# Gated delta attention and soft mixture on one core: biases forward, dispatch ahead, combination weights turned by DMA and in half precision

## The chip, the core and the metric

The kernel runs on one core of one Trainium2 chip. TensorE multiplies and transposes, VectorE, ScalarE and GpSimd work elementwise, SyncE issues DMAs. The metric is the device time of one execution in microseconds (us), here the median of three executions. Sources and views of the profile shorten the engines to PE, DVE, ACT, POOL and SP.

## The reference, cut to what matters

The input x is 4 x 2048 x 256. Two layers follow one another, each with a residual.

```python
# 1: gated delta attention on layernorm(x); per token, state S is 128 x 128
q, k, v = xn @ Wq + bq, normed(xn @ Wk + bk), xn @ Wv + bv
a, b, g = sigmoid(xn @ Wa + ba), sigmoid(xn @ Wb + bb), sigmoid(xn @ Wg + bg)
S = S @ (a * (I - b * k k^T)) + b * v k^T ;  o = (q S) * g ;  x1 = x + o @ Wo + bo
# 2: soft mixture on layernorm(x1), rms-normed: xn (2048 x 256), slots se (1024 x 256)
logits   = xn @ se.T                         # per batch 2048 x 1024
dispatch = softmax(logits, over tokens) ;    slots = dispatch.T @ xn
P        = gelu(slots @ w1) @ w2             # 1024 x 256
combine  = softmax(logits, over slots) ;     out = x1 + combine @ P
```

## The kernel before, in words

Everything is float32 in meaning. Wide products are made of half-precision pairs: each operand is split in a high and a low half-precision part, and three products (high x high, high x low, low x high) are summed in PSUM.

**Attention.** Tokens are taken in 16 chunks of 128, all four batches together. A step of the software pipeline (`step(i, q)`, run for i from -4) does the last work on chunk i and earlier work on chunks i+1 to i+4. A 16 x 16 diagonal part of each chunk's system is solved on VectorE by 15 pairs of small instructions (`product` L569, `column` L580), on data that go out to DRAM and come back (`M_dram`, `Mrep`, on SyncE's queue). Between the pairs, `biases` (L532) move the projections of chunk i+3 from PSUM into SBUF; TensorE's `queries` (L1060) and ScalarE's key norms wait for all four of them. At pair 10 `weights` (L614) makes PT, which TensorE's `heads` (L1176, L1177) wait for; ScalarE's `keys` (L879) wait for `heads`, and from them come the system matrix and the next DMA.

**Mixture.** Four batches run one after the other. Per batch TensorE does, in this order: logits of the first 512 slots (16 tiles of 128 tokens, `first_half`), logits of the second 512; `dispatch` of the first and of the second 512 slots (16 tiles each, 12 matmuls of 257 columns a tile, L1811); the two-layer expert (`hidden` L1837, `processed` L1851) for slot halves 0 and 1; then the combination: per tile of 128 tokens 8 transposes (`turn`, L1862) and 24 matmuls (`combine`, L1873). ScalarE copies each logits tile to L (L1620); VectorE updates the column maxima (L1457) and makes the row maxima (L1459). For dispatch, a tile passes VectorE (`shifted` L1481: L minus the column maxima, into Dm), ScalarE (`exps` L1640), ScalarE (`high_exps` L1647) and VectorE (`low` L1489). `turn_maxima`/`column_maxima`/`spread_maxima` reduce the column maxima and spread them over partitions, through TensorE, VectorE and TensorE again.

For the combination, ScalarE takes the exponential of a float32 row tile of L (`weights` L1680, into Ec), TensorE turns it in float32 into two PSUM banks, ScalarE copies the high half-precision part out (`high` L1686, Th), and VectorE subtracts for the low part (`low_weights` L1579, Tl). VectorE's `finish` (L1585, L1589) divides by the sum and adds x1. The x1 tiles and the results travel on SyncE's queue (`results`, L1402 to L1412), behind the reload of the dispatch operand X for the next batch (`load_X`, 32 DMAs).

The order of the work on each engine is written out by hand; there is no scheduler.

## Time and profile before

| | us |
|---|---|
| three executions | 1281.29, 1282.22 (median), 1282.69 |
| profiled execution | 1286.53 |
| its span, first to last instruction | 1284.7 |
| mean granted clock of TensorE | 0.977 of full speed |
| TensorE matmul busy | 1175.3 (91%) |
| VectorE busy / ScalarE busy / GpSimd busy | 906.5 / 727.6 / 240.9 |

Attention takes the first 509 us or so, and from one step to the next 27.5 us pass; the four batches of the mixture take 193.4, 193.2, 193.6 and 195.5 us. GpSimd is at work in the attention alone. Busy shares overlap, and an engine's mean is an average over stages with different limits, so the stage has to be read.

### The profile page before, as it was taken

To read this page: it belongs to the slowest core of one execution; us is meant where nothing else is said; L and a number is where in the kernel's file an instruction comes from. 1 tells how busy PE (TensorE), PEld (TensorE's weight loads), DVE (VectorE), ACT (ScalarE), POOL (GpSimd) and SP (SyncE) were. 2 spreads that over 40 slices of the span, in tenths; PEclk is the share of its full clock that TensorE was granted. 3 is DMA by queue.
4 is the path that set the end of the run, shared out by engine and by line. 5 is a ranking of instruction groups with operands and counts; after the bars stand their busy time and mean duration, and the time that the engine had idled before them with its cause. 6 is when DMAs were issued, how large, how long until landed. Compare 5 with 4: busy or idle time off the path is not lost.

```text
span 1284.7 us, 26863 instructions
## 1 busy us (share of the span) xinstructions
PE 1175.3 (91%) x8600; PEld 894.9 (70%) x8600; DVE 906.5 (71%) x2131; ACT 727.6 (57%) x1369; POOL 240.9 (19%) x275
## 2 busy tenths in 40 slices
PE   3599889989999978999999999999999999999999
PEld 2377767777777766467788467788467788466788
DVE  4568778888878874998445998445998445997444
ACT  3445555655555623578654478654478654477654
POOL 3445544556544540000000000000000000000000
PEclk9789999999999987999999999999999999999999
DMA  5113332232332124330212030212030212000012
GB/s 176 35 35 79 88 84 66 66 75 75 91 91 66 51 69 96 94 73 17 59 54 70 1 66 15 60 54 70 1 66 13 62 50 74 8 2 1 1 50 73
DMA packets 122044, 73.09 MB, mean 57 GB/s; under 512 B 50048, under 2 KB 119680, under 8 KB 121984
## 3 DMA queue, kind: packets, MB, share of 16 engines
q1 hardware_dynamic: 120656, 71.74, 20.7%
q8 instruction: 41, 0.67, 0.2%
q10 hardware_dynamic: 1264, 0.53, 0.2%
q14 instruction: 19, 0.16, 0.0%
q0 software_dynamic: 64, 0.00, 0.0%
HBM read 38.16 MB, written 25.69 MB: 50 GB/s over the span
## 4 chain that ended last, share of the span: by engine, by line
PE 47%; DVE 17%; issue 12%; DMA 8%; ACT 5%; SPq 4%; DVEq 1%; POOL 1%; ACTq 0%; POOLq 0%
PE m_wide L1873 13%; DMA Mrep<-M_dram 7%; PE m_wide L1851 7%; PE m_wide L1837 6%; SPq L285 4%; PE m_wide L1862 4%; PE m_wide L1758 4%; DVE m_Dm L1481 4%; DVE rmax L1459 2%; DVE cmax L1457 2%; ACT m_Eh L1647 2%; PE m_wide L1811 2%; DVE Zc L580 2%; DVE m_El L1489 2%; PE a_bank L1060 2%
## 5 line engine op out<-in xcount | busy, mean ns | idle before, releaser
L1811 PE MATMUL m_wide<-m_X,m_Eh 128*128 (+1 forms) x1024 | 172.5, 273 | 16.5 <-DVE m_El L1489 16.4
L1758 PE MATMUL m_wide<-seT,XT 128*128 128x512 f16 x672 | 147.3, 379 | 0.8 <-issue 0.8
L1873 PE MATMUL m_wide<-m_Ph,m_Th 128*128 128x257 f16 x512 | 140.4, 274 | 1.7 <-DVE m_Pl L1520 1.7
L1811 PE MATMUL m_wide<-m_X,m_El 128*128 128x257 f16 (+1 forms) x512 | 139.7, 273 | 0.0
L1873 PE MATMUL m_wide<-m_Ph,m_Tl 128*128 128x257 f16 x512 | 139.4, 272 | 0.0
L1873 PE MATMUL m_wide<-m_Pl,m_Th 128*128 128x257 f16 x512 | 139.1, 272 | 0.0
L1579 DVE TENSOR_TENSOR m_Tl<-m_wide,m_Th 128x1024 f16<-128x1024 f32 x64 | 78.4, 1224 | 71.4 <-ACT m_Th L1686 70.9
L1811 PEld LDWEIGHTS m_wide<-m_X,m_Eh 128*128 128x128 f16 x1024 | 97.7, 98 | 40.0 <-DVE m_El L1489 19.7
L1758 PEld LDWEIGHTS m_wide<-seT,XT 128*128 (+1 forms) x672 | 65.6, 98 | 78.1 <-issue 1.1
L1686 ACT CAST m_Th<-m_wide 128x1024 f16<-128x1024 f32 x64 | 64.7, 1011 | 86.1 <-PE m_wide L1862 86.1
L1620 ACT COPY L<-m_wide 128x512 f32 (+1 forms) x112 | 65.4, 587 | 84.3 <-PE m_wide L1758 84.0
L1640 ACT ACTIVATE m_E<-m_Dm,m_eshift 128x512 f32<-128x512 f32 x128 | 92.0, 722 | 31.8 <-DVE m_Dm L1481 30.6
L1489 DVE TENSOR_TENSOR m_El<-m_E,m_Eh 128x512 f16<-128x512 f32 x128 | 87.6, 687 | 9.5 <-ACT m_Eh L1647 5.9
L1481 DVE TENSOR_TENSOR m_Dm<-L,m_Mb 128x512 f32<-128x512 f32 x128 | 86.8, 684 | 1.4 <-ACT m_E L1640 1.4
L1851 PE MATMUL m_wide<-w2s,m_hh 128*128 128x256 f16 x512 | 84.3, 273 | 0.0
L1457 DVE TENSOR_TENSOR cmax<-cmax,L 128x512 f32<-128x512 f32 x112 | 77.0, 688 | 6.3 <-ACT L L1620 5.3
L1837 PE MATMUL m_wide<-m_sTh,w1s 128*128 128x512 f16 x256 | 77.6, 379 | 0.8 <-ACT m_E L1657 0.8
L1514 DVE TENSOR_TENSOR m_hl<-m_E,m_hh 128x512 f16<-128x512 f32 x64 | 43.6, 691 | 48.2 <-ACT m_hh L1668 48.2
L1647 ACT CAST m_Eh<-m_E 128x512 f16<-128x512 f32 x128 | 76.5, 604 | 0.0
L1459 DVE TENSOR_REDUCE rmax<-L (+1 forms) x112 | 75.9, 678 | 0.0
L1680 ACT ACTIVATE m_Ec<-L,m_nrm 128x1024 f32 (+1 forms) x64 | 73.6, 1150 | 0.3
L1851 PE MATMUL m_wide<-w2s,m_hl 128*128 128x256 f16 x256 | 69.8, 273 | 0.0
(187 smaller groups left out, 2628.5 us busy)
## 6 DMA issues: line engine op xcount, KB each, us to landing
L<-in_L_attn_x_dram SPq DMA_DIRECT2D x16, 512.0 KB, 7.4
Mrep<-M_dram SPq DMA_DIRECT2D x16, 512.0 KB
x_dram<-x SPq DMA_DIRECT2D x16, 512.0 KB, 7.4
m_X<-X_dram SPq DMA_DIRECT2D x128, 64.0 KB, 1.8
m_x1t<-x_dram SPq DMA_DIRECT2D x64, 128.0 KB, 2.1
out_dram<-m_o SPq DMA_DIRECT2D x64, 128.0 KB, 1.7
X_dram<-Xh SPq DMA_DIRECT2D x16, 256.0 KB, 2.3
X_dram<-Xl SPq DMA_DIRECT2D x16, 256.0 KB, 2.3
```

The lines of the kernel that those rows point to most:

```text
L1457: dve.tensor_tensor(cmax[:, half_at], cmax[:, half_at], L[:, z, bass.ds(tile, 1), :] .rearrange("q a n -> q (a n)"), ALU.max).then_inc(cm_ ...
L1459: dve.tensor_reduce(rmax[:, bass.ds(z * NT + tile, 1)], L[:, z, bass.ds(tile, 1), :] .rearrange("q a n -> q (a n)"), AX.X, ALU.max, negate ...
L1481: dve.tensor_tensor(Dm[p][:, :], L[:, v, bass.ds(4 * g + t, 1), :] .rearrange("q a n -> q (a n)"), Mb[:, v * HS:(v + 1) * HS], ALU.subtrac ...
L1489: dve.tensor_tensor(El[t % 4][:, :], E[t % 4][:, :], Eh[t % 4][:, :], ALU.subtract)\
L1579: dve.tensor_tensor(Tl[p][:, :], tp[p][:, :], Th[p][:, :], ALU.subtract).then_inc(Tl_ok[p], 1)
L1640: act.activation(E[t % 4][:, :], Dm[p][:, :], ACT.Exp, bias=eshift[:, 0:1]).then_inc(E_ok[p], 1)
L1647: act.copy(Eh[t % 4][:, :], E[t % 4][:, :]).then_inc(Eh_ok[p], 1)
L1758: last = pe.matmul(lg[t % 4], XT[:, sx * KD + k, bass.ds((4 * g + t) * P, P)], seT[:, ss, k, z * HS:(z + 1) * HS], start=(c == 0), stop=(c ...
L1811: last = pe.matmul(acc[v][q], e[t % 4][:, qs], X[:, sx, bass.ds(4 * g + t, 1), 0:XW].rearrange("q a n -> q (a n)"), start=first and e is E ...
L1837: last = pe.matmul(up[f % 2], w1s[:, sw, k, f * P:(f + 1) * P], sT[ss][:, k, :], start=(c == 0), stop=(c == 3 * KD - 1))
L1851: last = pe.matmul(down[q % 2], hT[sh][:, f, q * P:(q + 1) * P], w2s[:, sw, f, :], start=(c == 0), stop=(c == 3 * NF - 1))
L1873: last = pe.matmul(co[p], a[p][:, es], pp[:, e, 0:XW], start=(c == 0), stop=(c == 3 * NS - 1))
```

## The change: what it does

- **Attention.** The `biases` for b=3 and b=1 move from pair 7 to behind pairs 2 and 4. The third level of the block solve makes only the 64 x 64 corner that is used. Several semaphores become one.
- **Logits and dispatch.** VectorE's row maxima of the last 8 tiles of the second half (`LATE`) move into `hidden_low(0)`, behind the dispatch. In the place they leave, `shifted`, `exps`, `high_exps` and `low` of the first dispatch tiles are made. `turn_maxima(0)` and `spread_maxima(0)` move from tiles 1 and 3 to tiles 3 and 6. The two dispatch halves join without a restart: `shifted(1, ...)` runs two tiles ahead over the seam.
- **Combination.** The exponential is taken in place in L. VectorE's `split_weights` makes the high part Wh (a copy) and the low part Wl (a subtraction), both in SBUF and in half precision. Wh is turned by one DMA transpose a tile, 128 x 1024, SBUF to SBUF, on SyncE's queue into Th (four buffers; the four Wh lie over the room of Eh and El). Wl is turned on TensorE by 8 half-precision transposes, into one PSUM bank, and ScalarE copies it to Tl. The first four tiles' exponentials and splits are made between the expert's halves; this adds two activation table loads a batch. `combine(k, t)` now also waits for the DMA (`T_in`).
- **Plain transfers.** x1 (now 256 KB for two tiles) and results (128 KB a tile) are issued from GpSimd.

TensorE in the combination loop, before: the end of one tile's matmuls, the transposes, and the start of the next tile's (m_Ec the float32 weights, m_Th and m_Tl their turned parts, m_Ph and m_Pl the expert's output).

```order
L1873 MATMUL m_wide<-m_Ph,m_Tl 128x257
L1859 ISA
L1862 MATMUL m_wide<-ident,m_Ec 128x128 [waits m_Tl_ok0,m_Ec_ok0]
L1862 MATMUL m_wide<-ident,m_Ec 128x128 x7
L1873 MATMUL m_wide<-m_Ph,m_Th 128x257 [waits m_o_ok1,m_Tl_ok1]
L1873 MATMUL m_wide<-m_Pl,m_Th 128x257
```

The same place now (m_Wl the half-precision low part).

```order
L1952 MATMUL m_wide<-m_Ph,m_Tl 128x257
L1937 ISA
L1940 MATMUL m_wide<-ident,m_Wl 128x128 [waits m_Tl_ok0,m_Wl_ok]
L1940 MATMUL m_wide<-ident,m_Wl 128x128 x7
L1952 MATMUL m_wide<-m_Ph,m_Th 128x257 [waits m_o_ok1,m_T_in1,m_Tl_ok1]
L1952 MATMUL m_wide<-m_Pl,m_Th 128x257
```

The order is the same; the transposes read a half-precision tile, and the next tile's matmuls wait for the DMA transpose too.

VectorE near the end of the second-half logits, before: two tiles' maxima, then the first low part and the next shift of the dispatch.

```order
L1456 REGISTER_ALU [waits a_L_ok0]
L1457 TENSOR_TENSOR cmax<-cmax,L 128x512 [waits a_cm_ok]
L1459 TENSOR_REDUCE rmax<-L 128x1
L1456 REGISTER_ALU [waits a_L_ok1]
L1457 TENSOR_TENSOR cmax<-cmax,L 128x512 [waits a_cm_ok]
L1459 TENSOR_REDUCE rmax<-L 128x1
L1489 TENSOR_TENSOR m_El<-m_E,m_Eh 128x512 [waits m_Eh_ok0]
L1480 REGISTER_ALU
L1481 TENSOR_TENSOR m_Dm<-L,m_Mb 128x512 [waits m_E_ok0]
```

The same stage now, three tiles into the late ones.

```order
L1504 REGISTER_ALU [waits a_L_ok0]
L1505 TENSOR_TENSOR cmax<-cmax,L 128x512 [waits a_cm_ok]
L1533 ISA
L1534 TENSOR_TENSOR m_Dm<-L,m_Mb 128x512 [waits m_E_ok0]
L1504 REGISTER_ALU [waits a_L_ok1]
L1505 TENSOR_TENSOR cmax<-cmax,L 128x512 [waits a_cm_ok]
L1534 TENSOR_TENSOR m_Dm<-L,m_Mb 128x512 [waits m_E_ok1]
```

Each late tile has its column maximum and, in the place of its row maximum, one dispatch instruction.

ScalarE between the expert's two halves, before: the last hidden tile, the turned slots of half 1 (m_sTh) and the first results of half 0 (m_Ph); two more results follow.

```order
L1668 CAST m_hh<-m_E 128x512 [waits m_hf_ok1]
L1651 CAST m_sTh<-m_wide 128x1024 [waits m_sT_ps]
L1672 ISA
L1673 CAST m_Ph<-m_wide 128x256 [waits m_dn_ps0]
L1673 CAST m_Ph<-m_wide 128x256 [waits m_dn_ps1]
L1672 REGISTER_ALU
```

The same place now.

```order
L1721 CAST m_sTh<-m_wide 128x1024 [waits m_sT_ps]
L1747 ACT_TABLE_LOAD
L1747 ACTIVATE L<-L,m_nrm 128x2x512 [waits m_A_dve]
L1747 ACTIVATE L<-L,m_nrm 128x2x512
L1741 ISA
L1742 CAST m_Ph<-m_wide 128x256 [waits m_dn_ps0]
L1747 ACTIVATE L<-L,m_nrm 128x2x512
L1742 CAST m_Ph<-m_wide 128x256 [waits m_dn_ps1]
L1747 ACTIVATE L<-L,m_nrm 128x2x512
L1741 REGISTER_ALU
L1742 CAST m_Ph<-m_wide 128x256 [waits m_dn_ps0]
L1799 ACT_TABLE_LOAD
```

Four exponentials of 1024 columns (L1747) and two table loads stand before and between the copies of the results.

The diff, cut to its core:

```diff
-            if s == 7:
-                if live(i + 3):
-                    biases(i + 3, r, 3)
...
-            if s == 7:
+            if s == 2:
+                if live(i + 3):
+                    biases(i + 3, r, 3)
+            if s == 4:
                 if live(i + 3):
                     biases(i + 3, r, 1)
...
-                last = pe.matmul(bank[4][:, bs], M[q][0:HP, b, :], ZT[0:HP, bs], start=True, stop=True)
+                last = pe.matmul(bank[4][HP:, bs], M[q][0:HP, b, HP:], ZT[0:HP, bs], start=True, stop=True)
...
+Eh_room, El_room = sb("Eh", [P, 4 * HS], F16), sb("El", [P, 4 * HS], F16)
+Eh = [Eh_room[:, u * HS:(u + 1) * HS] for u in range(4)]
+El = [El_room[:, u * HS:(u + 1) * HS] for u in range(4)]
+Wh = [Eh_room[:, 0:E_SLOTS], Eh_room[:, E_SLOTS:], El_room[:, 0:E_SLOTS], El_room[:, E_SLOTS:]]
...
-Ec = two("Ec", [P, E_SLOTS])
-Th = two("Th", [P, E_SLOTS], F16)
+Wl = [sb(f"Wl{u}", [P, E_SLOTS], F16) for u in range(4)]
+Th = [sb(f"Th{u}", [P, NS, P], F16) for u in range(4)]
...
-tp = wide[0:2]
+tp = [wide[p][:, 0:E_SLOTS // 2].bitcast(F16) for p in range(2)]
...
-    def results(b):
...
-                sp.dma_start(x1t[p][:, :], x1_dram[bass.ds(b, 1), bass.ds(h * 2 * P + p * P, P), :]
...
-                sp.dma_start(out[bass.ds(b, 1), bass.ds(h * 2 * P + p * P, P), :]
...
+    def turn(b, k, t):
...
+        sp.wait_ge(co_ps[t % 2], n)
...
+        sp.wait_ge(Wh_ok, m)
...
+        sp.dma_start_transpose(Th[t][:, :, :], Wh[t]).then_inc(T_in[t], 16)
+
+    def turns(b):
+        for t in range(4):
+            turn(b, 0, t)
+        with sp.Fori(0, QB - 1) as k:
+            for t in range(4):
+                turn(b, k + 1, t)
...
+    def residuals(b, k, u, first=False):
...
+            pool.wait_ge(o_ok[1], n)
+        pool.sem_inc(going, 1)
+        pool.dma_start(x1t[u][:, :, :], x1_dram[bass.ds(b, 1), bass.ds(at, 2 * P), :]
...
+    def result(b, k, t):
...
+        pool.wait_ge(o_ok[p], n)
+        pool.sem_inc(going, 1)
+        pool.dma_start(out[bass.ds(b, 1), bass.ds(at, P), :]
...
+    with pool.Fori(0, B) as b:
+        residuals(b, 0, 0, first=True)
+        with pool.Fori(0, QB - 1) as k:
+            residuals(b, k, 1)
+            for t in range(2):
+                result(b, k, t)
+            residuals(b, k + 1, 0)
+            for t in range(2, 4):
+                result(b, k, t)
+        residuals(b, QB - 1, 1)
+        for t in range(4):
+            result(b, QB - 1, t)
...
-    def maxima(b, z, g, t):
+    def columns(b, z, g, t):
...
+    def rows(z, g, t):
...
+                if v == 0:
+                    rows(1, (LATE + f) // 4, (LATE + f) % 4)
+
+        def row_shifts():
+            dve.wait_ge(rm_ok, 2 * NT * nb)
+            dve.tensor_tensor(rmin[:, :], rmax[:, 0:NT], rmax[:, NT:], ALU.min).then_inc(rmin_ok, 1)
+            dve.wait_ge(rmin_ok, nb)
+            dve.tensor_scalar(nrm[:, :], rmin[:, :], ESHIFT, None, ALU.add).then_inc(A_dve, 1)
...
+        def split_weights(k, t):
+
+            row = L[:, :, bass.ds(4 * k + t, 1), :].rearrange("q z a n -> q z (a n)")
+            m, done = b * QB + k + 1, b * NT + 4 * k + t + 1
+            dve.wait_ge(Ec_ok, done)
+            dve.wait_ge(T_in[t], 16 * m)
+            dve.tensor_copy(Wh[t].rearrange("q (z n) -> q z n", z=2), row).then_inc(Wh_ok, 1)
+            dve.wait_ge(Wh_ok, done)
+            dve.wait_ge(tp_ps[t % 2], b * HB + 2 * k + t // 2 + 1)
+            dve.tensor_tensor(Wl[t][:, :].rearrange("q (z n) -> q z n", z=2), row,
+                              Wh[t].rearrange("q (z n) -> q z n", z=2), ALU.subtract).then_inc(Wl_ok, 1)
...
+        for t in range(LATE):
+            columns(b, 1, t // 4, t % 4)
+            rows(1, t // 4, t % 4)
+            if t == 3:
                 column_maxima(0)
         dve.wait_ge(Mb_ok, 2 * b + 1)
-
-        for t in range(2):
-            shifted(0, 0, t)
-        with dve.Fori(0, NT // 4 - 2) as g:
+        for t in range(LATE, NT):
+            columns(b, 1, t // 4, t % 4)
+            if t < LATE + 4:
+                shifted(0, 0, t - LATE)
+            elif t == LATE + 4:
+                low(0, 0, 0)
+            elif t == LATE + 5:
+                shifted(0, 0, 4)
+            elif t == LATE + 6:
+                low(0, 0, 1)
+        low(0, 0, 2)
+        shifted(0, 0, 5)
+        low(0, 0, 3)
+
+        for t in range(4, NT):
+            if t + 2 < NT:
+                shifted(0, 0, t + 2)
+            else:
+                if t + 2 == NT:
+                    dve.wait_ge(Mb_ok, 2 * b + 2)
+                shifted(1, 0, t + 2 - NT)
+            low(0, 0, t)
+            if t == 7:
+                column_maxima(1)
+        with dve.Fori(0, 2) as g:
             for t in range(4):
-                maxima(b, 1, g + 1, t)
...
         hidden_low(0)
+        row_shifts()
         slots_low(1)
-        processed_low(0)
+        processed_low(0, range(2))
+        split_weights(0, 0)
+        processed_low(0, range(2, QS))
+        split_weights(0, 1)
         hidden_low(1)

...
-            dve.tensor_tensor(Tl[p][:, :], tp[p][:, :], Th[p][:, :], ALU.subtract).then_inc(Tl_ok[p], 1)
...
-        low_weights(0, 0)
-        processed_low(1)
-        low_weights(0, 1)
-        with dve.Fori(0, HB - 1) as h:
-            for p in range(2):
-                finish(h, p)
-                low_weights(h + 1, p)
-        for p in range(2):
-            finish(HB - 1, p)
+        processed_low(1, (0,))
+        split_weights(0, 2)
+        processed_low(1, (1,))
+        split_weights(0, 3)
+        processed_low(1, (2, 3))
+        with dve.Fori(0, QB - 1) as k:
+            for t in range(4):
+                finish(k, t)
+                split_weights(k + 1, t)
+        for t in range(4):
+            finish(QB - 1, t)
...
-            act.activation(Ec[p][:, :].rearrange("q (z n) -> q z n", z=2), L[:, :, bass.ds(2 * h + p, 1), :].rearrange("q z a n -> q z (a n)"),
...
+        def weights(k, t):
+
+            row = L[:, :, bass.ds(4 * k + t, 1), :].rearrange("q z a n -> q z (a n)")
+            act.activation(row, row, ACT.Exp, bias=nrm[:, bass.ds(4 * k + t, 1)]).then_inc(Ec_ok, 1)
...
             act.wait_ge(tp_ps[p], n + 1)
-            act.copy(Th[p][:, :], tp[p][:, :]).then_inc(Th_ok[p], 1)
-
-        for t in range(4):
+            act.wait_ge(co_ps[p], n + 1)
+            act.copy(Tl[p][:, :], tp[p]).then_inc(Tl_ok[p], 1)
+
+        for t in range(LATE):
...
         maxima_out(0)
-        with act.Fori(0, NT // 4 - 2) as g:
+        for t in range(LATE, NT):
+            logits_out(b, 1, 0, t)
+            if t in (LATE + 1, LATE + 2):
+                exps(0, 0, t - LATE - 1)
+            elif t in (LATE + 3, LATE + 5, LATE + 7):
+                high_exps(0, 0, (t - LATE - 3) // 2)
+            elif t in (LATE + 4, LATE + 6):
+                exps(0, 0, (t - LATE) // 2)
+        exps(0, 0, 4)
+        high_exps(0, 0, 3)
...
-        act.wait_ge(A_dve, nb)
-        weights(0, 0)
+        act.activation(table[:, 1:2], zero[:, :], ACT.Gelu)
         hidden_high(0)
         slots_high(1)
-        processed_high(0)
+        act.wait_ge(A_dve, nb)
+        for t in range(2):
+            weights(0, t)
+        for q in range(QS):
+            processed_high(0, q)
+            if q < 2:
+                weights(0, q + 2)
+            elif q == 2:
+                act.activation(table[:, 1:2], zero[:, :], ACT.Gelu)
         hidden_high(1)
-        high(0, 0)
-        act.activation(table[:, 1:2], zero[:, :], ACT.Exp)
-        weights(0, 1)
-        processed_high(1)
-        with act.Fori(0, HB - 1) as h:
-            for p in range(2):
-                weights(h + 1, p)
-                high(h + p, 1 - p)
-        high(HB - 1, 1)
+        low_turned(0, 0)
+        for q in range(QS):
+            processed_high(1, q)
+        act.activation(table[:, 0:1], zero[:, :], ACT.Exp)
+        low_turned(0, 1)
+        with act.Fori(0, QB - 1) as k:
+            for t in range(4):
+                weights(k + 1, t)
+                low_turned(k + (t + 2) // 4, (t + 2) % 4)
+        for t in range(2, 4):
+            low_turned(QB - 1, t)
...
+        for t in range(LATE):
             logits(b, 1, 0, t)
-            if t == 1:
+            if t == 3:
                 for p in range(2):
                     pe.wait_ge(Tl_ok[p], HB * b + 1)
                 turn_maxima(0)
-        spread_maxima(0)
-        with pe.Fori(0, NT // 4 - 1) as g:
+            elif t == LATE - 2:
+                spread_maxima(0)
+        with pe.Fori(LATE // 4, NT // 4) as g:
             for t in range(4):
-                logits(b, 1, g + 1, t)
+                logits(b, 1, g, t)
...
-                last = pe.transpose(tp[p][:, e * P:(e + 1) * P], Ec[p][:, e * P:(e + 1) * P], ident[:, :])
+                last = pe.transpose(tp[p][:, e * P:(e + 1) * P], Wl[t][:, e * P:(e + 1) * P], ident16[:, :])
             last.then_inc(tp_ps[p], 1)
...
+            pe.wait_ge(T_in[t], 16 * (b * QB + k + 2))
...
-                for a, pp in ((Th, Ph), (Th, Pl), (Tl, Ph)):
-                    last = pe.matmul(co[p], a[p][:, es], pp[:, e, 0:XW], start=(c == 0),
-                                     stop=(c == 3 * NS - 1))
+                for a, pp in ((Th[t][:, e, :], Ph), (Th[t][:, e, :], Pl), (Tl[p][:, es], Ph)):
+                    last = pe.matmul(co[p], a, pp[:, e, 0:XW], start=(c == 0), stop=(c == 3 * NS - 1))
...
-        with pe.Fori(0, NT // 4 - 2) as g:
-            for t in range(4):
-                dispatch(0, g + 1, t)
-        for t in range(NT - 4, NT):
+        for t in range(4, NT):
             dispatch(0, 0, t)
-            if t == NT - 4:
+            if t == 9:
                 spread_maxima(1)
```

## Rows read from the trace of the kernel before

**Rows 1.** Busy time by engine in stretches of one batch: whole, then three parts.
```profile
702.40:895.60 193.20, 187.41 (x1410) 138.15 (x1409) 132.97 (x223) 117.82 (x177) 0.00 (x0) 1.00 0.16 44
723.50:746.70 23.20, 21.98 (x104) 10.15 (x104) 21.65 (x37) 13.37 (x24) 0.00 (x0) 1.00 0.01 1
746.70:772.20 25.50, 22.59 (x200) 19.30 (x200) 23.73 (x42) 20.66 (x36) 0.00 (x0) 1.00 0.39 83
772.20:796.10 23.90, 22.83 (x201) 19.11 (x202) 20.96 (x38) 19.33 (x31) 0.00 (x0) 1.00 0.00 1
```

**Rows 2.** Chain that ended last: sixteen tiles of first-half logits, and two dispatch tiles; start, us.
```profile
702.60 20.72 PE m_wide L1758 x96
...
793.62 2.64 PE m_wide L1811 x24
```

**Rows 3.** Chain that ended last, combination: one tile's eight transposes, one tile's 24 matmuls.
```profile
650.61 0.87 PE m_wide L1862 x8
651.48 2.65 PE m_wide L1873 x24
```

**Rows 4.** TensorE in order of time, end of the attention: half-precision transposes.
```profile
502.61 0.61 PE L1201 MATMUL a_bank<-ident,L 128*128 128x128 f16 x8
```

**Rows 5.** Busy time by stretch around Rows 4; the value 1.00 is the granted clock.
```profile
502.50:503.20 0.70, 0.70 (x11) 0.53 (x9) 0.39 (x1) 0.33 (x2) 0.00 (x0) 1.00 0.00 0
```

**Rows 6.** Waits of TensorE in that batch: total us, times, longest.
```profile
PE m_wide L1811 <- DVE m_El L1489: 4.1, 8, 1.5
PE m_wide L1789 <- DVE m_mcol L1474: 1.0, 1, 1.0
```

**Rows 7.** Groups of VectorE instructions: count | busy us, mean ns of one | idle before.
```profile
L1481 DVE TENSOR_TENSOR m_Dm<-L,m_Mb 128x512 f32<-128x512 f32 x128 | 86.8, 684 | 1.4 <-ACT m_E L1640 1.4
...
L659 DVE TENSOR_TENSOR Xl<-xf,Xh 128x1024 f16<-128x1024 f32 x16 | 31.3, 1957 | 0.9 <-ACT Xh L941 0.9
...
L1589 DVE SCALAR_TENSOR_TENSOR m_o<-m_wide,m_cden,m_x1t 128x256 f32<-128x256 f32 x64 | 31.0, 484 | 7.9 <-DMA m_x1t<-x_dram 6.0 <-DVE m_cden L1585 0.8
...
L676 DVE CAST w1s<-L 128x2048 f16<-128x2048 f32 x1 | 1.2, 1201 | 0.0
```

**Rows 8.** Groups of ScalarE instructions: exponentials of the combination, and activation table loads.
```profile
L1680 ACT ACTIVATE m_Ec<-L,m_nrm 128x1024 f32 x56 | 64.5, 1151 | 0.3
...
L1657 ACT ACT_TABLE_LOAD x4 | 5.1, 1283 | 2.0 <-PE m_wide L1837 2.0
```

**Rows 9.** ScalarE in order of time, between the two hidden layers of one batch.
```profile
808.18 1.01 ACT L1651 CAST m_sTh<-m_wide 128x1024 f16<-128x1024 f32 x1
810.15 0.37 ACT L1673 CAST m_Ph<-m_wide 128x256 f16<-128x256 f32 x1 [0.96 <-PE m_wide L1851]
812.77 0.37 ACT L1673 CAST m_Ph<-m_wide 128x256 f16<-128x256 f32 x1 [2.25 <-PE m_wide L1851]
```

**Rows 10.** VectorE in order of time, one attention step.
```profile
331.99 0.42 DVE L532 SCALAR_TENSOR_TENSOR L<-a_bank,bkv 128x258 f32<-128x258 f32 x1
...
333.81 0.68 DVE L614 TENSOR_TENSOR PT<-a_bank,gamb_ 128x512 f32<-128x512 f32 x1
```

**Rows 11.** TensorE in order of time, the same step.
```profile
333.87 0.65 PE L1076 MATMUL a_bank<-a_const,ab 128*128 128x128 f32 x4
...
334.64 0.46 PE L1176 MATMUL a_bank<-qTg_,S 128*128 128x128 f32 x2
```

**Rows 12.** Who waited for whom on ScalarE, whole run.
```profile
ACT kh_ L879 <- PE a_bank L1177: 11.0, 14, 1.0
```

**Rows 13.** DMA transposes of the run: issue time ns min/median/max, and time to landing.
```profile
L322 SPq DMA_TRANSPOSE XT<-X_dram x6: 1174/1248/3918, 480.0 to 522.1; - x6
...
L1390 SPq DMA_TRANSPOSE XT<-X_dram x6: 3902/4143/4323, 562.4 to 953.6; - x6
...
DMA to landing us min/median/max: 2.3/6.2/8.9
```

**Rows 14.** SyncE's DMA queue in order of time: reload of the dispatch operand.
```profile
796.73 24.86 SPq L1398 DMA_DIRECT2D m_X<-X_dram  x32
```

More of the change, by code:

```diff
@@ L669, in mixture_weights @@
                                                  ALU.mult, ALU.mult)
[L670 removed]
+                    last.then_inc(w1_ok, 1)
                 elif step == 2:
@@ L1466, in first_half @@
                     for t in range(4):
-                        maxima(b, 0, g, t)
+                        columns(b, 0, g, t)
+                        rows(0, g, t)
             def batch(b):
@@ L1569, in batch @@
+                for t in range(8, NT):
+                    if t + 2 < NT:
+                        shifted(1, 0, t + 2)
+                    low(1, 0, t)
+                    if t < 8 + QS:
+                        slots_out(0, [t - 8])
                 slots_low(0)
@@ L1694, in batch @@
+                exps(0, 0, 4)
+                high_exps(0, 0, 3)
+                for t in range(4, NT):
+                    if t + 1 < NT:
+                        exps(0, 0, t + 1)
+                    else:
+                        exps(1, 0, 0)
+                    high_exps(0, 0, t)
+                    if t == NT - 3:
+                        maxima_out(1)
+                with act.Fori(0, NT // 4 - 1) as g:
                     for t in range(4):
-                        logits_out(b, 1, g + 1, t)
+                        exps(1, g, t + 1)
+                        high_exps(1, g, t)
@@ L1750, in _ @@
                 pe.sem_inc(tp_ps[p], 1)
+                pe.sem_inc(co_ps[p], 2)
+            for u in range(4):
+                pe.sem_inc(T_in[u], 16)
             def logits(b, z, g, t):
@@ L1791, in spread_maxima @@
                     last.then_inc(Mb_ps, 1)
-                for t in range(4):
+                for t in range(LATE):
                     logits(b, 1, 0, t)
-                    if t == 1:
+                    if t == 3:
                         for p in range(2):
@@ L1912, in batch @@
                     pe.wait_ge(Pl_ok[p], cut_to)
-                with pe.Fori(0, HB - 1) as h:
-                    for p in range(2):
-                        combine(h, p)
-                        turn(h + 1, p)
-                for p in range(2):
-                    combine(HB - 1, p)
+                with pe.Fori(0, QB - 1) as k:
+                    for t in range(4):
+                        combine(k, t)
+                        turn(k + (t + 2) // 4, (t + 2) % 4)
+                for t in range(4):
+                    combine(QB - 1, t)
+                    if t < 2:
+                        turn(QB - 1, t + 2)
             with pe.Fori(0, B - 1) as b:
```

197 lines of the change are left out of this document (73 added, 124 removed).

## Prediction

> **What bounds the kernel now.** I read the page's 40 slices first: TensorE is near nine tenths nearly everywhere, and the slices divide the run into an attention up to about 509 us and four like batches of the mixture. Then the busy time by stretch of one batch [rows 1]: 193.2 us, of which TensorE is busy 187.4, at a granted clock of 1.00. So a batch is TensorE's own work plus a few us of holes, and an edit is worth something only if it shortens TensorE's work or fills a hole. The chain of waits gives the true rates, since busy times of pipelined matmuls overlap: 96 logits matmuls take 20.72 us, two dispatch tiles (24 matmuls) 2.64 [rows 2]; in the combination a tile costs 2.65 for 24 matmuls and 0.87 for eight transposes, 3.52 together [rows 3].
>
> With these rates the holes of a batch can be placed. Second-half logits: 20.7 plus two sets of four float32 transposes (2 x 0.43) are 21.6, against a stretch of 23.2: 1.6 us of hole. First dispatch: 16 tiles are 21.1, with two such sets 22.0, against 25.5: 3.5. Second dispatch: 21.1 and 0.87 for the turned slots, 22.0, against 23.9: 1.9 [rows 1, 2]. The list of waits names 1.0 for the transposed column maxima (L1789) and 4.1 for VectorE's low parts (L1811) [rows 6].
>
> The attention is different: there a chain through VectorE, TensorE, ScalarE and a DMA comes round once in 27.5 us (the start of a step to the start of the next), and TensorE waits in it.
>
> **The change, part by part.**
>
> *Transposes of the combination.* 64 tiles x 8 float32 transposes go, 64 x 8 half-precision ones come. Eight of these took 0.61 us from first start to last end at clock 1.00 [rows 4, 5]; that includes the tail of the last one, which in a chain lies under what follows, so I take 0.45 a tile. The saving is 0.42 (bounds: nothing, if a set costs 0.87 as now; 0.26 with the whole 0.61). 16 x 0.42 = 6.7 a batch, **-27 us** in all.
>
> Is a tile then 3.10 us on TensorE, or is something slower? ScalarE: exponential 1.15 [rows 8] and a copy of 1024 columns like the one at 808.18, 1.01 [rows 9]: 2.2. VectorE: the division about 0.2, sum 0.48, a copy of 1024 columns at half of the 1201 ns of L676, 0.60, and a subtraction of 1024 columns, twice the 512 of L1481, at most 1.37, so 2.65 and some waiting on itself [rows 7]. SyncE: one DMA transpose a tile. No transpose out of SBUF is in the trace. From DRAM, one of 128 rows (64 KB) occupies the queue 1.17 us and one of 2048 rows (1 MB) 4.14; landing takes 2.3 to 8.9 [rows 13]. A 256 KB one lies between them, 1.17 to 4.14; by size 1.8, which I take. It has time: the four buffers let tile k+4 be turned while three tiles (9.7 us) run. The first four also have room, since the reload of X ends at 821.6 [rows 14] and the combination starts at 841.
>
> *Dispatch prepared ahead.* VectorE's instructions of 512 columns last 0.68 [rows 7]. Eight row maxima leave the logits stage and sit in the hidden layer, where VectorE has one such instruction for every 1.3 us of TensorE. In their place seven dispatch instructions come, so dispatch can begin without waiting. I take all of the 1.0 for the column maxima, which are now asked for three tiles after they were turned; 3.2 of the 3.5 in the first dispatch, the start and the seam; and 1.4 of the 1.9 in the second, where four inserted divisions (0.6 each) lengthen VectorE's tile but now find it ahead. 5.6 a batch, **-22 us** (bounds: 0 to 7.0 a batch).
>
> *Exponentials and table loads between the expert's halves.* This costs. ScalarE is free at 809.2 [rows 9], loads a table (1.28 [rows 8]), by then has the row shifts (one row maximum, 0.68, and two tiny instructions behind the last low part), and does two exponentials: 810.7 + 2.25 = 812.9. Only then comes the copy that stood at 810.15, then VectorE's low part (0.4): 813.7. TensorE's third chunk needs that bank, and would start at about 812.5, when the copy at 812.77 shows the second chunk done [rows 9]. Hole 1.2 a batch, **+5 us** (0 to 2.5, if the table is loaded only after the shifts). The second table load before hidden(1) lies within a chunk's 2.6 us; the third exists today.
>
> *Biases earlier.* They end 1.1 us earlier in a step, since three pairs of small instructions no longer stand ahead. This starts `queries` and the spread of alpha earlier, but `heads` wait for PT too. PT is made at pair 10, behind the same work as before: it ends at 333.81 + 0.68 = 334.49; alpha's four transposes start at 333.87 and end about there; `heads` start at 334.64 [rows 10, 11]. ScalarE's keys wait for `heads` 14 times [rows 12]. The two roads meet with no slack between them, so shortening one leaves PT as the last: gain 0 to 0.1 a step. **-1 us** (bounds 0 and 13 x 1.1 = 14, if PT were not the last). The smaller corner matmul has as many columns to stream and counts 0.
>
> *Transfers on GpSimd.* It is idle in the mixture, and a result has two tiles, 6 us, to leave. In the loop 0; the last result goes by another queue, **+1 us** (0 to 3).
>
> Sum: -27 -22 +5 -1 +1 = -44. On the profiled execution's 1286.5 that is 1242.5; it stands 4.3 above the median of the runs shown (its span is 1284.7, the rest 1.8 lies around it), so on the median's scale 1282.2 - 44 = **1238**.
>
> **A rule against the trace.** Rows 13 and the 1 MB in 4.14 us say that transposes from DRAM move some 250 GB/s, so 256 KB need about 1 us of the DMA engines. The Trainium skill, page "Advanced Engine Details and Errata", section "X-Bar Transpose (TRN2)", says the same in words: transposing DMAs are as fast as regular ones. By that rule the queue stays hidden and the sum stands. But the page "DMA: Bandwidth & Descriptors" of the Trainium skill, section "Why a DMA increments its semaphore by 16 and not by 1", gives for SBUF to SBUF on earlier generations 262,144 sequencer cycles for 8,192 tiles, one push a tile: 32 cycles each. It doesn't say how large a tile is; with SyncE at 1.2 GHz (the skill's first page) an estimate is 1.7 us for 64 tiles of 4 KB, hidden, and 6.8 us for 256 tiles of 1 KB, which would be the first rival below. No run here shows it yet.
>
> **The rivals.**
>
> *The transposes out of SBUF hold up the combination (slower).* Let one cost T on SyncE's queue, one after the other. Four are made ahead; the fifth starts 4.2 us into the loop (one tile's matmuls, division, copy), twelve follow, the last lands 1.1 behind its issue (2.3 less 1.17 [rows 13]), and 2.65 of matmuls follow: 8.0 + 12 T. Forecast is 16 x 2.65 + 14 x 0.45 = 48.7. From T = 3.4 it decides; at T = 4.14 the loop is 57.7, +36 us, 1274; above T = 4.3 the 44 us are eaten and the kernel is slower; at 6.2, the median landing, one at a time, it is +135, 1373. For: source in SBUF is unseen, and plain transfers were cleared off this queue. Against: bytes and rates of rows 13. Chance 0.24.
>
> *VectorE becomes the bound of the combination.* L659, 1024 columns with both inputs in SBUF while GpSimd works, lasts 1.957 [rows 7], not 1.37. With GpSimd's transfers beside it a tile would be 0.7 + 0.9 + 1.96 and waits, 3.7, 0.6 over TensorE: 14 x 0.6 x 4 = +33, 1271. Against: GpSimd only issues. Chance 0.08.
>
> *The half-precision transposes or the preparation give half.* If loading weights keeps the eight transposes near 0.7, or dispatch still starts with a hole, 10 to 25 us are missing: about 1255. Chance 0.09.
>
> *The attention shortens by all of 1.1 a step.* For: TensorE does wait for the biases today. Against: PT. 1238 - 13 = 1225. Chance 0.07.
>
> *The forecast*, 1226 to 1252, has 0.52.
>
> **How the numbers follow.** The low end lies at the forecast's own, 1226, and leaves 0.05 of the attention's case out. The high end, 1305, takes in all cases but the slower one, and of that the part with T up to about 4.8; 0.14 is left out above. The likeliest case's own range is 1226 to 1252. A change of 0.2% (2.6 us) is what a measurement of this kernel can tell. Faster by more: 0.52 + 0.08 + 0.09 + 0.07 less a little for T near 4.3, 0.74; within it 0.02; slower 0.24.
>
> **What the profile will show.** Right: on TensorE a combination tile every 3.1 us with no wait for m_Th; dispatch starting within 0.3 us of the last logits; one hole of about 1.2 us at the third chunk of processed(0); attention steps still 27.5 us, with TensorE's `heads` waiting on PT and `queries` starting about 1.1 earlier. Wrong: SyncE's transposes lasting over 3.1 us each, m_Wh copies waiting for T_in or matmuls for the landing; VectorE back to back in the combination; attention steps under 27.

## The result, and the profile after

Four executions of the changed kernel took 1255.7, 1263.6, 1267.3 and 1269.5 us, median 1265.5, against 1282.5 of the kernel before in the same comparison: ratio 0.986 (0.983 to 0.989), 17 us less where 44 were forecast. Run again five times it took 1258.6 (1254.3 to 1265.3) against 1281.2, 22.5 less. Its first four executions also spread over 14 us.

The profiled execution is the fastest of these, 1255.7 us with a span of 1254.0. Its busy times by stretch for the second batch answer to [rows 1]: whole, second-half logits, dispatch.

```profile
695.10:880.10 185.00, 179.93 (x1411) 131.68 (x1409) 142.35 (x239) 120.28 (x181) 14.64 (x24) 1.00 0.31 69
715.90:738.70 22.80, 21.86 (x105) 10.26 (x105) 19.90 (x34) 14.26 (x25) 0.00 (x0) 1.00 0.01 3
738.70:784.00 45.30, 44.67 (x402) 38.87 (x401) 41.50 (x71) 38.70 (x64) 0.00 (x0) 1.00 0.24 47
```

The batch takes 185.0 instead of 193.2; the two dispatches 45.3 instead of 49.4; TensorE has 0.6 us without work there. The chain of waits in the combination answers to [rows 3]: a tile is 0.45 + 2.65 = 3.10 us, and nothing is waited for between.

```profile
834.22 0.45 PE m_wide L1940 x8
834.66 2.65 PE m_wide L1952 x24
837.31 0.45 PE m_wide L1940 x8
```

The waits of TensorE in the whole mixture (total us, times, longest):

```profile
PE m_wide L1952 <- DVE m_Pl L1581: 10.5, 4, 2.7
PE m_wide L1929 <- DVE m_Pl L1581: 3.3, 4, 0.8
PE m_wide L1866 <- DVE m_mcol L1527: 2.4, 3, 0.9
PE m_wide L1889 <- DVE m_El L1542: 2.2, 10, 0.3
```

Dispatch (L1889) waited 4.1 us in one batch [rows 6], now 2.2 in four. The 3.3 at L1929 belong to the forecast hole in the first processed layer. The 10.5 at L1952 were not forecast: in each batch TensorE stands 2.7 us before the first combination tile (before: 1.7 us in all four). VectorE in order of time at that place shows why; the bracket is the idle time and what ended it:

```profile
637.18 0.68 DVE L1590 CAST m_El<-L 128x1024 f16<-128x1024 f32 x1
642.19 1.23 DVE L1593 TENSOR_TENSOR m_Wl<-L,m_El 128x1024 f16<-128x1024 f32 x1 [4.33 <-PE m_wide L1940]
643.33 0.75 DVE L1581 TENSOR_TENSOR m_Pl<-m_wide,m_Ph 128x256 f16<-128x256 f32 x2
```

VectorE could have subtracted tile 3's weights at 637.9. It waits 4.33 us for TensorE's transposes of tile 1 (L1940), which TensorE issues only behind the whole processed layer. Queued behind that wait are the last two low parts of the expert's output (L1581), and for them TensorE waits. The granted clock shows a second cost. Two stretches of the first batch, then the same two of the second:

```profile
642.20:645.70 3.50, 0.96 (x9) 0.86 (x10) 1.88 (x3) 3.30 (x4) 0.00 (x0) 1.00 0.00 0
646.10:649.40 3.30, 3.30 (x21) 2.53 (x19) 0.22 (x2) 0.00 (x0) 0.00 (x0) 0.50 0.00 0
827.70:831.10 3.40, 1.03 (x14) 0.81 (x11) 1.89 (x3) 2.75 (x5) 0.00 (x0) 1.00 0.00 0
832.00:835.40 3.40, 3.40 (x38) 3.03 (x36) 0.90 (x3) 0.86 (x2) 0.00 (x0) 1.00 0.02 5
```

Behind the hole the first batch runs 3.4 us at 0.50, which is 1.2 GHz, the second at 1.00; the combination took 50.33 and 48.68 us. So a half-clock stretch costs 1.65 us.

The DMA transposes, one line of issues (ns min/median/max), and time to landing, against [rows 13]:

```profile
L1415 SPq DMA_TRANSPOSE m_Th<-m_Eh x32: 1232/1239/1288, 623.0 to 1233.0; - x32
...
DMA to landing us min/median/max: 3.0/3.6/5.1
```

One takes 1.24 us of the queue for 256 KB, under the 1.8 of the forecast.

In the attention, VectorE and GpSimd in order of time in one middle step (first product at 243.8), against [rows 10]:

```profile
248.85 0.45 DVE L580 TENSOR_TENSOR Zc<-Zc,tmp 128x28 f32<-128x28 f32 x1
249.34 0.18 DVE L569 TENSOR_TENSOR tmp<-Mrep,Zc 128x24 f32<-128x24 f32 x1
...
249.90 0.68 DVE L614 TENSOR_TENSOR PT<-a_bank,gamb_ 128x512 f32<-128x512 f32 x1
```

```profile
248.22 1.04 POOL L418 TENSOR_TENSOR L<-a_const,ab 128x512 f32<-128x512 f32 x1 [6.37 <-ACT ab L865]
```

and TensorE, against [rows 11]:

```profile
248.25 0.60 PE L1076 MATMUL a_bank<-a_const,ab 128*128 128x128 f32 x4
250.73 0.46 PE L1176 MATMUL a_bank<-qTg_,S 128*128 128x128 f32 x2 [1.89 <-DVE PT L614]
```

`queries` and alpha do come earlier, and `heads` now wait 1.89 us for PT: that PT would be last was forecast. Two things were not. TensorE has one long hole there, and one column instruction takes 0.45 us, ending 0.04 behind GpSimd's L418; in the other steps it takes 0.35 and 0.45 in turn. Before, the same instruction and L418 stood like this in the step of [rows 10], with L418 starting only under PT (L614):

```profile
333.08 0.17 DVE L580 TENSOR_TENSOR Zc<-Zc,tmp 128x28 f32<-128x28 f32 x1
```

```profile
333.89 1.04 POOL L418 TENSOR_TENSOR L<-a_const,ab 128x512 f32<-128x512 f32 x1 [8.23 <-ACT ab L865]
```

### The profile page after: what moved, and what is told of

Read it like the earlier page. It is cut to its first block, busy times and chain, and to the rows that moved or that the text cites. A ratio compares the mean times of both kernels' runs of the same rounds, so it can differ in the third digit from the quotient of the medians.

```text
span 1254.0 us, 26991 instructions
## 1 busy us (share of the span) xinstructions
PE 1138.2 (91%) x8600; PEld 862.8 (69%) x8600; DVE 949.4 (76%) x2195; ACT 737.6 (59%) x1385; POOL 299.9 (24%) x373
## 4 chain that ended last, share of the span: by engine, by line
PE 42%; DVE 23%; issue 10%; DMA 9%; ACT 6%; SPq 5%; DVEq 0%; POOL 0%; ACTq 0%; POOLq 0%
PE m_wide L1952 14%; DMA Mrep<-M_dram 8%; PE m_wide L1835 7%; PE m_wide L1929 5%; SPq L285 5%; PE m_wide L1915 4%; DVE m_Dm L1534 3%; DVE tmp L569 2%; PE m_wide L1940 2%; DVE Zc L580 2%; DVE m_El L1542 2%; DVE cmax L1505 2%; DVE rmax L1511 2%; ACT m_Eh L1717 2%; PE m_wide L1889 2%
## 5 line engine op out<-in xcount | busy, mean ns | idle before, releaser
L1472 POOL DMA_DIRECT2D out_dram<-m_o x64 | 35.5, 555 | 639.6 <-DVE m_o L1656 636.5
L1889 PE MATMUL m_wide<-m_X,m_Eh 128*128 128x257 f16 (+1 forms) x1024 | 171.1, 273 | 2.3 <-DVE m_El L1542 2.2
L1952 PE MATMUL m_wide<-m_Ph,m_Th 128*128 128x257 f16 x512 | 141.7, 277 | 10.5 <-DVE m_Pl L1581 10.5
L1952 PE MATMUL m_wide<-m_Ph,m_Tl 128*128 128x257 f16 x512 | 140.7, 275 | 0.0
L1952 PE MATMUL m_wide<-m_Pl,m_Th 128*128 128x257 f16 x512 | 140.4, 274 | 0.0
L1889 PE MATMUL m_wide<-m_X,m_El 128*128 128x257 f16 (+1 forms) x512 | 139.7, 273 | 0.0
L1889 PEld LDWEIGHTS m_wide<-m_X,m_Eh 128*128 128x128 f16 x1024 | 99.2, 98 | 19.6 <-issue 3.5
L1690 ACT COPY L<-m_wide 128x512 f32<-128x512 f32 (+1 forms) x112 | 65.2, 585 | 77.0 <-PE m_wide L1835 76.2
L1753 ACT COPY m_Tl<-m_wide 128x1024 f16<-128x1024 f16 x64 | 64.7, 1011 | 75.5 <-PE m_wide L1940 75.5
L1929 PE MATMUL m_wide<-w2s,m_hh 128*128 128x256 f16 x512 | 84.8, 273 | 3.3 <-DVE m_Pl L1581 3.3
L1511 DVE TENSOR_REDUCE rmax<-L 128x1 f32<-128x512 f32 (+1 forms) x112 | 76.1, 679 | 0.0
L1747 ACT ACTIVATE L<-L,m_nrm (+1 forms) x64 | 73.2, 1150 | 0.9 <-DVE m_nrm L1576 0.9
L1929 PE MATMUL m_wide<-w2s,m_hl 128*128 128x256 f16 x256 | 69.8, 273 | 0.0
```

Source lines behind the costliest of these rows:

```text
L1511: dve.tensor_reduce(rmax[:, bass.ds(z * NT + tile, 1)], L[:, z, bass.ds(tile, 1), :] .rearrange("q a n -> q (a n)"), AX.X, ALU.max, negate ...
L1747: act.activation(row, row, ACT.Exp, bias=nrm[:, bass.ds(4 * k + t, 1)]).then_inc(Ec_ok, 1)
L1889: last = pe.matmul(acc[v][q], e[t % 4][:, qs], X[:, sx, bass.ds(4 * g + t, 1), 0:XW].rearrange("q a n -> q (a n)"), start=first and e is E ...
L1929: last = pe.matmul(down[q % 2], hT[sh][:, f, q * P:(q + 1) * P], w2s[:, sw, f, :], start=(c == 0), stop=(c == 3 * NF - 1))
L1952: last = pe.matmul(co[p], a, pp[:, e, 0:XW], start=(c == 0), stop=(c == 3 * NS - 1))
```

## The experiments

Two measures help in the traces. The middle of the attention is twelve steps, from about 130 to 460 us. Each runs from VectorE's first product to the next one and is split where VectorE makes M (L559): the DMA part from there to the next product, and the rest. The other measure is the start of the first batch's second-half logits, called the start of the mixture here; the first half, 21 us, lies ahead of it. Medians are of 5 or 6 executions, of 12 in experiment 4. Experiments 5, 6, 8 and 10, and then 7, 9 and 11, were run on two other chips than 1 to 4; the kernel before took 1281.2, 1281.9 and 1280.4 us on the three, so medians of different chips compare to about 1 us.

**1. The same kernel again.**

> The changed kernel once more, unchanged, for a second trace of it. Its profiled execution took 1255.7 us, the other three 1263.6 to 1269.5, with a granted clock of 0.966 to 0.970 instead of 0.973. Theory 1 (hole and clock): the 10 us lie in stretches at half clock, each set off by a hole of TensorE, above all the one of 2.65 us before the combination's first tile. Then a slower execution shows more than two of its four combinations with a stretch at half clock (1.65 us each) and more of them elsewhere. Theory 2 (late DMA transposes): a slower execution shows combine matmuls waiting for the landing, combinations well over 50.3 us, and no more stretches at half clock. Theory 3: the attention is what varies, from 509 us to over 515.

1258.6 us. The traced execution is again the fastest of its five (1254.3), so no slow execution of this kernel was seen from inside. Two of four combinations began at half clock and took 50.34 and 50.50 us, the others 48.68. Outside these, every stage of the mixture repeats to 0.4 us, most to 0.1. No matmul of a combination waited for a DMA: theory 2 falls. The mixture started at 528.3 us here, at 529.4 in the first trace, and at 536.1 and 532.4 in two traces below with the same attention (experiments 2 and 4): what varies is the attention (theory 3) and the clock (theory 1).

**2. The wait before the combination.**

```diff
-dve.wait_ge(tp_ps[t % 2], b * HB + 2 * k + t // 2 + 1)
+dve.wait_ge(tp_ps[t % 2], b * HB + 2 * k + t // 2 + (0 if first and t > 1 else 1))
```

`first` is set for tiles 2 and 3 of the four made between the expert's halves.

> The changed kernel with one wait shortened: in the first four tiles VectorE's low part of tile 2 and 3 waited until the tile two before had been turned, which its buffer doesn't need; it waits for one turning less. So VectorE is free for the last two low parts of the expert's output, which stood behind it. Theory 1: the hole before the combination falls from 2.65 us to about 1, 4 x 1.7 = 7 us, and the half-clock stretches at its start go too, another 3 to 7: 10 to 14 us under the changed kernel, median about 1253, and less spread. Theories 2 and 3: 7 us and the spread stays.

1248.9 us, 9.8 less. TensorE's wait fell from 10.5 to 4.2, and VectorE no longer stops ahead of the last low parts:

```profile
PE m_wide L1952 <- DVE m_Pl L1581: 4.2, 4, 1.1
```

```profile
644.57 1.23 DVE L1593 TENSOR_TENSOR m_Wl<-L,m_El 128x1024 f16<-128x1024 f32 x1
646.13 0.42 DVE L1581 TENSOR_TENSOR m_Pl<-m_wide,m_Ph 128x256 f16<-128x256 f32 x1 [0.34 <-ACT m_Ph L1742]
```

From processed(1) to the combination 12.17 us instead of 13.75, 6.3 in the four batches, and no combination at half clock. Over all traces of the changed kernels: 13 of 24 combinations behind a 2.7 us hole began at half clock, none of 20 behind 1.1. With 1.65 each, 2.2 a run, that is 3.6 more: 9.9, for 9.8 measured.

**3. Attention as before.**

> The changed kernel with the attention as before (the biases of b=3 and b=1 back at pair 7, the third level's product 128 rows high). As predicted: attention steps have PT as the last thing, so moving the biases gained 0 to 0.1 us a step: within 2 us of the changed kernel. Rival: the move gained up to 1.1 us a step and is hidden by something in the trace: this one is 5 to 14 us slower. If the earlier biases cost something (theory 3), it is faster and spreads less.

1249.5 us (1244.7 to 1252.2), 9.1 less than the changed kernel (1254.3 to 1265.3), no overlap. The term for the attention, -1, is thus wrong: its change cost 9 us. This edit also takes back the smaller corner product; experiment 8 separates the two.

**4. Dispatch order as before.**

> The changed kernel with logits and dispatch ordered as before on VectorE, ScalarE and TensorE (no late row maxima, no dispatch tiles made ahead); combination, attention and transfers as changed. From the traces a batch's logits and dispatch took 0.7 and 4.1 us less in the changed kernel, so this one should be 4 x 4.8 = 19 us slower less what returns at the third chunk of the first processed layer, where the row shifts are then ready earlier (up to 4 x 1.1): 15 to 19 us slower, about 1282. As the prediction had it (5.6 a batch): 22. If the preparation is not what shortened the dispatch, nothing.

1278.5 us, 19.8 slower, a little above the expected 15 to 19, and TensorE's wait for low parts is back:

```profile
PE m_wide L1897 <- DVE m_El L1542: 16.3, 31, 1.5
```

The first processed layer takes 11.38 us instead of 11.61, so of the 1.1 that might have come back with the row shifts made earlier only 0.2 did: the row shifts are not what holds the third chunk.

**5. Both single edits.**

> The changed kernel with both single edits that made it faster: attention as before (biases back at pair 7) and the shortened wait of VectorE before the combination. Alone they brought 1258.6 to 1249.5 and to 1248.9. If the two causes are separate (one hole of TensorE in every attention step, another before each combination), they add: 1258.6 - 9.1 - 9.8 = about 1240. If both medians only came from the same thing, say one lucky chip, this one stays near 1249.

1240.25 us: the two causes add. Undoing the attention's change on top of the shortened wait gives 8.6 us, so its cost is seen twice.

**6. Filling the hole before `heads`.**

```diff
+for b in [0, 1, 2, 3] * 3:
+    pe.transpose(by_batch[2][:, b, :], ident, ident)
 pe.wait_ge(qTg_ok, c + 1)
 pe.wait_ge(PT_ok, c + 1)
```

> The changed kernel, biases forward as in it, with twelve useless float32 transposes (about 1.3 us of TensorE) in each attention step between alpha's transposes and the wait of heads for PT, into a bank that heads overwrite. In the traces TensorE idles there 1.6 us a step since the biases went forward, and in 9 of 48 middle steps a stretch at half clock began within 2 us behind it (1 of 24 with the biases at pair 7); such a step is 1.5 to 2 us longer. Theory 1 (the idle engine loses its clock): with the hole filled the stretches in the middle of the attention go, and the kernel with more work is 6 to 9 us faster than the changed one, about 1251. Rival (the early biases cost through VectorE's order or its semaphores): no gain, 1258, or slower if the transposes delay heads.

1263.8 us, slower than the changed kernel. Theory 1 had 1251; the rival had 1258, or more if `heads` came later, but they start 0.83 us behind PT's start, as without the filler. The trace splits the time. The wait for PT fell to at most 0.6 us, and no middle step had a half-clock stretch. But the logits stages of the second and the third batch took 47.6 and 48.0 us instead of 43.4, with this in each:

```profile
718.67 4.88 PE L1837 MATMUL m_wide<-seT,XT 128*128 128x512 f16 x14 [3.40 <-issue]
```

A hole of 3.4 us (3.9 in the third batch) that nothing in the profile releases, behind the loop over the first half, and in each case a half-clock stretch with it. The added instructions lie before that loop in TensorE's program; that they shift how its code is fetched is argued, not shown. Less these 8.7 us it would be 1255.1.

**7. Filler with two instructions.** On the kernel with the shortened wait (1248.9).

```diff
+pe.matmul(bank[2][:, :], ident, const[:, 0:512], start=True, stop=True)
+pe.matmul(bank[2][:, 0:256], ident, const[:, 0:256], start=True, stop=True)
```

> The changed kernel with the shortened wait, biases forward, and two useless float32 matmuls of 512 and 256 columns (1.3 us) instead of twelve transposes ahead of the wait for PT: fewer instructions than in the first filler, whose middle attention lost all its half-clock stretches but whose batches 1 and 2 each had a hole of 3.4 us with no releaser at the start of the second-half logits. Theory 1: no half-clock stretch between 110 and 450 us, 13 x 0.34 = 4.4 us less than 1248.9, about 1244.5, unless the 3.4 us holes come again (then about 1253, and the trace shows them). Rival: the filler itself delays the step, and 1249 or more without such holes.

1247.5 us. Those holes did not come; again no half-clock stretch in twelve steps, and the rest of a step went from 13.43 to 13.17 us. The gain is 1.4 of the expected 4.4, and within the spread: the DMA part of the steps was 14.7 us in this trace, 14.4 in that without filler, so a whole step was not shorter (27.9 and 27.8 us). Whether the filler or chance did that stays open. So the traces show that the half-clock stretches go with the hole (9 of 48 steps with it, none of 24 with it filled), and no run shows a gain in time from filling it.

**8. One bias early, one late.**

> The changed kernel with only the biases of b=1 back at pair 7, those of b=3 stay behind pair 2. Queries wait for all four, so alpha starts about 1.1 us later than in the changed kernel and the idle time before heads falls from 1.6 to about 0.6 us. Theory 1: few or no stretches at half clock in the middle of the attention, median about 1250. Rival (each early bias costs by itself): half the loss, about 1254.

1251.9 us, halfway between theory 1 (1250) and the rival (1254), so the median does not decide. The trace does: the long column instruction is 0.17 again in every middle step, the rest of a step is 12.85 us, and one of the twelve steps has a half-clock stretch. This kernel keeps the smaller corner product, so that product has no visible part in the loss.

**9. GpSimd's order.** On the kernel with the shortened wait; GpSimd makes the key norms ahead of the spread of beta (L418).

> The changed kernel with the shortened wait (1248.9 us) and the biases forward, and on GpSimd the key norms of chunk i+3 ahead of the spread of beta (L418, 128 x 512 from two SBUF tiles, 1.04 us). With the biases forward L418 starts 4.47 us behind the first product instead of 5.85, and VectorE's small column instruction at 5.10, two SBUF inputs, lasts 0.45 instead of 0.17, to just behind the end of L418; PT stands 6.15 instead of 5.78 behind the first product. Theory (VectorE held by GpSimd's instruction): with L418 about 1.2 us later the column is 0.17 again and PT back at 5.8, 13 steps x 0.37 = 4.8 us, and with a hole before heads of 1.25 instead of 1.6 us fewer stretches at half clock: 1240 to 1244. Rival (the statistics or the place of the biases in VectorE's own order cost the 0.37): no change, 1249.

1252.8 us: neither the expected 1240 to 1244 nor the rival's 1249. Yet this is the run that shows the mechanism best. The twelve steps are of two sorts in turn. VectorE and GpSimd in one of the first sort:

```profile
255.52 0.18 DVE L569 TENSOR_TENSOR tmp<-Mrep,Zc 128x20 f32<-128x20 f32 x1
255.62 0.68 DVE L614 TENSOR_TENSOR PT<-a_bank,gamb_ 128x512 f32<-128x512 f32 x1
```

```profile
255.55 1.05 POOL L418 TENSOR_TENSOR L<-a_const,ab 128x512 f32<-128x512 f32 x1
```

and in one of the second:

```profile
283.31 1.01 DVE L569 TENSOR_TENSOR tmp<-Mrep,Zc 128x20 f32<-128x20 f32 x1
284.25 0.68 DVE L614 TENSOR_TENSOR PT<-a_bank,gamb_ 128x512 f32<-128x512 f32 x1
```

```profile
283.25 1.04 POOL L418 TENSOR_TENSOR L<-a_const,ab 128x512 f32<-128x512 f32 x1
```

VectorE's instruction 0.03 us ahead of L418 lasts 0.18; 0.06 us behind it, it lasts 1.01 and ends with it. The Trainium skill has a rule for this in its page "SBUF — State Buffer", section "SBUF: two separate sides": a VectorE operation with two SBUF inputs and a GpSimd operation that reads SBUF lock a shared port pair, and the one that starts second blocks until the first is over. The trace agrees with it for VectorE. Every long product or column instruction of this trace and of the changed kernel's ends 0.03 to 0.04 us behind an L418. That L418 is held when it starts second does not show: under VectorE's 0.18 us it lasts 1.05 instead of 1.04. The second sort's hole before `heads` is 2.5 us, and four of its five steps between 140 and 400 us had a half-clock stretch.

**10. Exponentials behind the copies.** On the kernel of 5.

```diff
-for t in range(2):
-    weights(0, t)
-for q in range(QS):
-    processed_high(0, q)
...
+act.activation(table[:, 0:1], zero[:, :], ACT.Exp)
...
+processed_high(0, 0)
+weights(0, 0)
+processed_high(0, 1)
+weights(0, 1)
+weights(0, 2)
+processed_high(0, 2)
+weights(0, 3)
+act.activation(table[:, 1:2], zero[:, :], ACT.Gelu)
+processed_high(0, 3)
```

> As the kernel with both edits, and between the expert's halves ScalarE copies the first two results before the first exponentials (table load, copy, exponential, copy, two exponentials, copy, exponential, table load, copy) instead of making two exponentials first. Predicted and seen hole at the third chunk of the first processed layer: 1.13 us in each batch. If the exponentials before the copy make it, it goes: 4 x 1.1 = 4.5 us less, about 1236. If another wait takes its place (the table load before the second hidden layer), it is even or slower.

1236.1 us, 4.2 less; processed(0) 10.61 us instead of 11.61.

**11. The last low parts waited for later.** On the kernel of 10.

```diff
+if t == 0:
+    for u in range(2):
+        pe.wait_ge(Pl_ok[u], cut_at)
...
 for e in range(NS):
+    if t == 0 and e >= NS - 2:
+        pe.wait_ge(Pl_ok[e % 2], cut_to)
...
-for p in range(2):
-    pe.wait_ge(Pl_ok[p], cut_to)
```

> The kernel with both edits and the copies ahead of the exponentials (1236.1 us), where TensorE in the first tile of each combination waits for the last two low parts of the expert's output only before the last two of its eight slot blocks, not before the whole combination. The 1.2 us hole that is left there should go: 4 x 1.2 = 4.8 us, about 1231.5. If the turned low weights of the tile (ScalarE's copy) come last anyway, half of it or nothing.

1234.4 us, ratio 0.964 (0.962 to 0.967): the fastest, 24 us under the changed kernel. In the trace the last hole is gone (10.93 instead of 12.17 before a combination, 4.9 in all, for 4.8 expected); the medians differ by 1.7, within their spread. TensorE's waits in the mixture that remain:

```profile
PE m_wide L1891 <- DVE m_El L1542: 1.8, 8, 0.3
PE m_wide L1868 <- DVE m_mcol L1527: 1.6, 3, 0.8
PE m_wide L1837 <- issue: 0.5, 1, 0.5
```

## Why the prediction was wrong, by its steps

| term | forecast | measured |
|---|---|---|
| half-precision transposes | -27 | -27: 0.87 to 0.45 each, 64 tiles |
| dispatch prepared ahead | -22 | -21 by the stages of all four batches, -19.8 by undoing it |
| hole in processed(0) | +5 | +4.5 |
| hole before the combination | none | +8.8: TensorE's wait 1.7 to 10.5 us in four |
| clock behind that hole | none | +3.6: about two stretches of 1.65 |
| biases earlier | -1 | +8.6 by the rests of the steps, +6.8 by whole steps, +9.1 by undoing it |
| last result | +1 | +1.4 |
| sum | -44 | -21, against -17.0 and -22.5 |

*Transposes, combination, queue: right.* A tile is 3.10 us, set by TensorE. VectorE's subtraction takes 1.23 us (forecast at most 1.37), SyncE's transpose 1.24 (1.8). Neither the slow transposes (chance 0.24) nor VectorE as the bound (0.08) came true. By the first rule weighed in the prediction, that transposing DMAs are as fast as regular ones (the Trainium skill, page "Advanced Engine Details and Errata", section "X-Bar Transpose (TRN2)"), the queue stays hidden, and it does; no run here compares the two kinds of DMA. The estimate of 6.8 us for 256 tiles, made from the Trainium skill's page "DMA: Bandwidth & Descriptors", section "Why a DMA increments its semaphore by 16 and not by 1", does not agree with 1.24.

*Dispatch: right in kind.* In the second batch 4.8 us instead of 5.6; the logits gained 0.7 where 1.0 was taken, the two dispatches 4.1 of 4.6. In all four batches together these stages are 20.7 us shorter, since the first batch's logits gained 1.9.

*Third chunk of processed(0): right*, 1.0 to 1.1 us where 1.2 was forecast; experiment 10 shows the exponentials ahead of the copy as the cause.

*What failed first: the step that placed the four early splits between the expert's halves at no cost on VectorE.* The prediction followed ScalarE's queue there, copy by copy, and not VectorE's. The code of `split_weights` waits for `tp_ps` and stands ahead of `processed_low(1, (2, 3))`; following who is queued behind that wait gives the 2.7 us. The wait was one count higher than its buffer needs.

*What failed second: "gain 0 to 0.1 a step".* PT is last, as said, and whole steps without a half-clock stretch stay near 27.5 us. But the bounds went from no gain to 14 us of gain and left a loss out: it was not asked what else starts 1.4 us earlier. GpSimd's spread of beta does (4.5 us behind the first product, before 5.9), and lands on a column instruction; VectorE's PT starts 0.42 us later behind the first product than before (6.19 instead of 5.77), and the small product and column instructions ahead of it are 0.33 of that longer in sum. The rest of a step goes from 12.77 us to 13.17. And the time that TensorE no longer waits before `queries`, it waits before `heads`, in one piece of up to 1.89 us:

| attention | half-clock stretches in the middle steps | rest of a step | whole step |
|---|---|---|---|
| biases at pair 7 (five traces) | 1 of 60 | 12.76 to 12.86 | 27.1 to 27.5 |
| biases forward (four) | 9 of 48 | 13.43 to 13.56 | 27.8 to 28.0 |
| forward, hole filled (two) | 0 of 24 | 13.17 | 27.7, 27.9 |
| forward, GpSimd's order changed | 4 of 12 | 13.70 | 28.1 |
| one bias forward | 1 of 12 | 12.85 | 27.5 |

0.40 for VectorE behind GpSimd and 0.26 for the clock, 13 steps: 8.6 us. Whole steps grew by less, 0.52 us in the mean or 6.8 in all, because the DMA part was some 0.15 shorter in the forward traces; no run shows why. The mixture started at 518.4 to 529.0 us in the five traces and at 528.3 to 536.1 in the four, so one pair of traces alone does not show the loss: the first two, before and after, have 529.0 and 529.4. The stretches come in some steps and not in others of the same program, which also makes the changed kernel's executions differ more.

*The range*, 1226 to 1305, holds both medians, but by luck as far as the cause goes: it was made wide for rivals of which none came true, and no rival held either of the two failed steps. The likeliest case's own range, 1226 to 1252, does not hold them. Without the two failed steps the forecast stands: the changed kernel with both undone takes 1240.25, for 1238 predicted.

## What to carry to other kernels

Where a change puts an instruction with a wait between others, read that engine's queue behind it to the next thing someone waits for, on every engine and not only on the one that looks busy; and check the count in the wait against what the buffer needs. Work moved forward off the critical path is not free: ask what starts earlier with it, and on which instruction of another engine that falls. A hole of TensorE is more than its length when its clock falls behind it, so two short holes can be better than a long one; here holes of 1.1 us never brought the half clock, and holes of 2.7 us did in about half of the cases.
